# A graph layer with routed experts: the table of normed nodes kept in plain fp32 instead of three bf16 parts

## The chip, the cores and the metric

The kernel runs on one core of one Trainium2 chip. The time is the device time of one launch, in microseconds (us). Before the change it is 1744.55 us, the median of three runs (1744.52 to 1745.57). One further execution was profiled; what the profile calls the span reaches from its first to its last instruction.

## The reference, cut to what matters

6250 nodes with 256 features each; 100,000 edges, sorted by destination; eight experts with 256 x 1024 and 1024 x 256 weights. All of it is fp32.

```python
def _layernorm(x, axis=-1, eps=1e-05):
    return (x - mean) / jnp.sqrt(var + eps)

def gnn(x, edge_index, weight, bias):          # x is the normed input
    src, dst = edge_index
    summed = segment_sum(x[src], dst, n)
    deg = segment_sum(ones(src), dst, n)
    agg = summed / jnp.maximum(deg, 1.0)[:, None]
    out = jnp.concatenate([x, agg], -1) @ weight
    return out / norm(out) + bias

def ffn(h):                                    # h is the normed x
    probs = softmax(h @ gate_w + gate_b); idx = argmax(probs)
    # each token goes to its expert's next free slot (capacity C),
    # relu(buf @ w1 + b1) @ w2 + b2, back to the token, times its gate
    ...

x = x + gnn(_layernorm(x), [src, dst], ...)
x = x + ffn(_layernorm(x))
```

## The kernel before

**Setup (about the first 129 us).** The 49 blocks of 128 nodes are normed in seven groups of seven. VectorE takes the statistics (L942 to L947), norms the group (L967) and writes into `r1` what is left of each value when its upper 16 bits are taken off (L973). The upper halves of `xn` and of `r1` are two bf16 parts, copied out by ScalarE (L531, L535); the third part is what is then left, computed by GpSimd (L443). SyncE stores the three parts of a group (L249, L278) in a table in DRAM, `parts_d`, of 6250 rows of 768 bf16 values (1536 bytes). In groups 1 and 2 the edge lists (L868 to L885) and the tables of the loop (L892 to L933) are made. GpSimd's gathers start when all stores have landed (L448).

**The loop.** 49 trips, each with four quads of edges. A quad is 512 edges: four tiles of 128. For each tile GpSimd gathers the 128 source rows into `ring` (L460, an indirect DMA), which holds two quads. VectorE makes the four 128 x 128 selection matrices of a visit in one instruction (L991): a 1 where an edge's destination is a given node of the block. A visit adds up a quad's edges for one block of nodes. On TensorE each of its four tiles takes four bf16 matmuls with the same `sel` tile as weights: three of 256 columns, one for each part (L684), and one of a single column of ones (L690), which counts the edges. VectorE adds the 257 sums to `acc` (L1000). A quad has one visit, and one more where its edges cross into another block; 244 visits in all, five in nearly every trip, the earlier ones of a quad in a loop of their own ahead of its last one.

**What lies between the visits.** After each tile of a quad's last visit TensorE runs one step of a plan written out by hand (L800): steps of the node block whose sums are complete (transposes L725, the 512 x 256 linear layer L738, transposes L774, gate L780, counts L789), and from trip 8 on steps of one chunk of 128 routed rows of an expert (L731, L747, L755, L766, all fp32). The first eight trips have no chunk; in them SyncE loads the experts' weights. After the 49 trips come the last node blocks and chunks, without quads.

**What orders it.** Each engine runs its program in order. `sel_ready` and `acc_done` let a visit start (L700 to L706), `gathered` lets each pair of tiles start (L682), `ring_free`, raised by the last matmul of each tile, lets GpSimd gather again (L457), and `visit_done`, raised by the last matmul of a visit, lets VectorE add and select again (L1020, L1029, L1034). `sel` and `ps_q` have two buffers. A visit that is not its quad's last uses the buffers of the visit before it. In VectorE's trip (L1237 and on) the chains of routing, expert result and new row follow these waits in order.

```python
for part in range(NPART):
    mm = pe.matmul(ps[:, 0:D], sel[:, s, j, :], ring[..., part * D:(part + 1) * D], ...)
if final:
    mm.then_inc(ring_free, 1)
mm = pe.matmul(ps[:, D:AW], sel[:, s, j, :], ones_bf[:, :], ...)
```

## Time and profile before

| | |
|---|---|
| Median of the runs | 1744.55 us |
| Span of the profiled execution | 1742.4 us |
| TensorE, matmul records | 1183.2 us busy, 68% |
| VectorE / ScalarE / GpSimd | 898.6 / 469.4 / 922.7 us busy |
| Mean granted TensorE clock | 0.898 of 2.4 GHz |
| Three stages: setup / 49 trips / the rest | to 129 / 129 to about 1550 / to 1742 us |

The profiled execution's span lies 2.2 us below the median of the runs. Busy time is the time covered by records of work; register, branch and semaphore instructions are not counted. An fp32 matmul stands in the records as two matmuls and two weight loads, a bf16 one as one of each. Starts of matmuls are measured, their ends are modelled, so matmuls are best priced by the distance from one start to the next.

### The profile page before, as it was taken

What the parts mean: (1) busy time and instruction counts of PE and PEld (TensorE: products, weight loads), DVE (VectorE), ACT (ScalarE), POOL (GpSimd) and SP (SyncE); (2) the same over time, 40 slices, a digit from 0 to 9 for tenths busy, and PEclk for the clock granted to TensorE, in tenths of its full rate; (3) what the DMA queues carried; (4) which work ended last, traced back from release to release, by engine and by line L of the source; (5) the groups of instructions that cost most, each with busy time, mean ns of one, the idle gap of its engine ahead of it and who ended that gap; (6) DMA issues with size and microseconds to landing.
All of it is one profiled execution on the core that took longest, in us unless ns stands there. A gap on an engine that the chain in (4) does not pass through costs nothing.

```text
span 1742.4 us, 32300 instructions
## 1 busy us (share of the span) xinstructions
PE 1183.2 (68%) x6813; PEld 838.8 (48%) x6814; DVE 898.6 (52%) x3823; ACT 469.4 (27%) x1362; POOL 922.7 (53%) x939
## 2 busy tenths in 40 slices
PE   0105566677777777777777776877677777777785
PEld 0004444455555555555555554645455655554553
DVE  5753444455555545454555554554555545554443
ACT  2221111122222222222222322223222222233432
POOL 4136656656666656555656655565556665640110
PEclk9998676789999989998989998999998899888998
DMA  7736667554545444544445444444454544431111
GB/s 236 235 134 205 185 215 232 185 160 131 147 136 146 135 131 132 149 121 134 136 118 139 126 138 115 134 127 140 114 143 121 146 120 137 124 103 34 38 42 38
DMA packets 126810, 238.77 MB, mean 137 GB/s; under 512 B 21263, under 2 KB 85126, under 8 KB 126792
## 3 DMA queue, kind: packets, MB, share of 16 engines
q0 software_dynamic: 55808, 160.87, 32.7%
q1 hardware_dynamic: 70984, 77.72, 14.1%
q14 instruction: 14, 0.11, 0.0%
q8 instruction: 4, 0.07, 0.0%
HBM read 207.46 MB, written 39.29 MB: 142 GB/s over the span
## 4 chain that ended last, share of the span: by engine, by line
PE 28%; issue 19%; DVE 17%; another core or an unknown queue 11%; DVEq 10%; DMA 7%; ACT 4%; POOL 2%; SPq 2%; ACTq 0%; POOLq 0%
PE ps_q L684 10%; PE ps_h L747 5%; PE ps_b L766 5%; PE ps_a L738 3%; DVEq L1252 3%; DVEq L1060 2%; DMA ring<-parts_d,idx 2%; DVE sel L991 2%; PE ps_a L725 2%; DMA b_b<-in_L_ffn_b 2%; DMA out<-ys,node_i 1%; PE ps_t L755 1%; DVE acc L1000 1%; ACT cat_t L580 1%
## 5 line engine op out<-in xcount | busy, mean ns | idle before, releaser
L460 POOL DMA_INDIRECT ring<-parts_d,idx x784 | 763.0, 973 | 541.1 <-PE ps_q L684 277.9
L684 PE MATMUL ps_q<-ring,sel 128*128 128x256 bf16 x2928 | 506.0, 299 | 245.0 <-DMA ring<-parts_d,idx 96.7
L684 PEld LDWEIGHTS ps_q<-ring,sel 128*128 128x128 bf16 x2928 | 270.4, 106 | 416.8 <-issue 242.2
L766 PE MATMUL ps_b<-w_sb,hid_t 128*128 x864 | 264.6, 441 | 124.2 <-issue 71.2
L991 DVE SCALAR_TENSOR_TENSOR sel<-lane,block,dst_t 128x512 bf16<-128x512 bf16 x245 | 184.4, 753 | 197.4 <-issue 116.2
L766 PEld LDWEIGHTS ps_b<-w_sb,hid_t 128*128 128x128 f32 x864 | 169.6, 214 | 161.6 <-issue 141.5
L747 PE MATMUL ps_h<-w_sb,hid_t 128*128 x432 | 213.6, 622 | 5.7 <-ACT hid_t L583 5.7
L1000 DVE TENSOR_TENSOR acc<-acc,ps_q 128x257 f32 x245 | 103.3, 422 | 178.3 <-issue 57.3
L690 PE MATMUL ps_q<-ones_bf,sel 128*128 128x1 bf16 x976 | 170.8, 175 | 0.0
L738 PE MATMUL ps_a<-gw_sb,cat_t 128*128 128x256 f32 x416 | 136.3, 459 | 19.3 <-ACT cat_t L580 15.6
L604 ACT ACTIVATE hid_t<-ps_t,b_t 128x128 f32<-128x128 f32 x432 | 117.8, 382 | 55.5 <-remote 40.1
L515 ACT ACTIVATE sm<-sm 128x1 f32<-128x1 f32 x104 | 21.1, 203 | 358.3 <-DVE sm L1113 192.0
L690 PEld LDWEIGHTS ps_q<-ones_bf,sel 128*128 128x128 bf16 x976 | 105.0, 108 | 21.0
L478 POOL DMA_INDIRECT out<-ys,node_i x55 | 57.2, 1041 | 108.6 <-DVEq L1060 94.9
L598 ACT ACTIVATE hid<-ps_h 128x512 f32<-128x512 f32 x108 | 62.5, 596 | 193.7 <-PE ps_h L747 142.1
L470 POOL DMA_INDIRECT disp_d<-row,slot x53 | 60.2, 1136 | 90.9 <-issue 53.1
L747 PEld LDWEIGHTS ps_h<-w_sb,hid_t 128*128 128x128 f32 x432 | 76.3, 195 | 66.2 <-issue 65.2
L738 PEld LDWEIGHTS ps_a<-gw_sb,cat_t 128*128 128x128 f32 x416 | 84.0, 223 | 35.3 <-ACT cat_t L580 20.5
L755 PE MATMUL ps_t<-ident,hid 128*128 128x128 f32 x432 | 69.5, 284 | 30.0 <-ACT hid L598 25.7
L755 PEld LDWEIGHTS ps_t<-ident,hid 128*128 128x128 f32 x432 | 46.8, 141 | 46.0 <-ACT hid L598 33.3
L580 ACT ACTIVATE cat_t<-ps_a 128x512 f32<-128x512 f32 x52 | 31.0, 597 | 129.8 <-remote 64.7
L591 ACT ACTIVATE hid_t<-ps_a 128x256 f32<-128x256 f32 x52 | 19.9, 383 | 161.6 <-PE ps_a L738 91.4
(180 smaller groups left out, 1296.1 us busy)
## 6 DMA issues: line engine op xcount, KB each, us to landing
w_sb<-in_L_ffn_w SPq DMA_DIRECT2D x32, 512.0 KB
ring<-parts_d,idx POOLq DMA_INDIRECT x784
disp_d<-row SPq DMA_DIRECT2D x1, 8450.0 KB
parts_d<-w_sb SPq DMA_DIRECT2D x6, 1344.0 KB, 5.8
xs<-disp_d SPq DMA_DIRECT2D x55, 130.0 KB
ys<-disp_d SPq DMA_DIRECT2D x55, 130.0 KB
b_b<-in_L_ffn_b SPq DMA_DIRECT2D x55, 128.0 KB
xb<-in_x SPq DMA_DIRECT2D x51, 128.0 KB
```

The source lines that it names most:

```text
L460: pool.indirect_dma_start(ring[:, (k % 2) * TQ + j, :], None, parts_d[:, :], bass.IndirectOffsetOnAxis(ap=idx[:, k * TQ + j:k * TQ + j + 1 ...
L470: pool.indirect_dma_start(disp_d[:, :], bass.IndirectOffsetOnAxis(ap=slot[0:rows, 0:1], axis=0), row[0:rows, :], None, bounds_check=EX * S ...
L598: act.activation(hid[:, h * 512:(h + 1) * 512], ps_h[:, h * 512:(h + 1) * 512], ACT.Copy).then_inc(hid_ready, 1)
L604: done = act.activation(hid_t[:, j, :], ps_t[:, j, :], ACT.Relu, bias=b1_t[:, ds(e * JF + j, 1)])
L684: mm = pe.matmul(ps[:, 0:D], sel[:, s, j, :], ring[:, (k % 2) * TQ + j, part * D:(part + 1) * D], start=(j == 0 and part == 0), stop=(j == ...
L690: mm = pe.matmul(ps[:, D:AW], sel[:, s, j, :], ones_bf[:, :], start=False, stop=(j == TQ - 1), skip_group_check=True)
L738: last_ = pe.matmul(ps_a[:, 0:KD, :], cat_t[:, k, :], gw_sb[:, k, :], start=(k == 0), stop=(k == 2 * KD - 1))
L747: last_ = pe.matmul(ps_h[:, h * 512:(h + 1) * 512], xc_t[:, k, :], w1_sb[:, k, ds(expert[0] * F + h * 512, 512)], start=(k == 0), stop=(k ...
L755: last_ = pe.transpose(ps_t[:, j, :], hid[:, j * P:(j + 1) * P], ident[:, :])
L766: last_ = pe.matmul(ps_b[:, 0:D], hid_t[:, j, :], w2_sb[:, j, ds(expert[0] * D, D)], start=(j == 0), stop=(j == JF - 1))
L991: dve.scalar_tensor_tensor(out=sel[:, s, :, :], in0=lane[:, :].rearrange("p (j m) -> p j m", j=1).to_broadcast((P, TQ, P)), scalar=block0[ ...
L1000: dve.tensor_tensor(to, to, ps_q[s][:, 0:AW], ALU.add).then_inc(acc_done, 1)
```

## The change

The table in DRAM becomes `xn_d`, 6250 rows of 256 fp32 values (1024 bytes), stored straight from `xn`. `r1`, the two copies of ScalarE and GpSimd's subtraction are gone, with their semaphores; VectorE waits for the store of two groups before (`xn_out`) ahead of norming into the same buffer. `ring` is fp32, 257 columns wide; the last column is set to 1.0 once. `sel` is fp32. A tile takes one fp32 matmul of 257 columns; the last tile of a visit takes one of 256 columns and a second one of one column, which ends the accumulation of the count. `acc` is cleared ahead of the loop on GpSimd without waits in between.

```diff
-    parts_d = nc.dram_tensor("parts_d", (N, NPART * D), BF16, kind="Internal").ap()
+    xn_d = nc.dram_tensor("xn_d", (N, D), FP32, kind="Internal").ap()
-        ring = sb("ring", [P, 2 * TQ, NPART * D], BF16)
+        ring = sb("ring", [P, 2 * TQ, AW], FP32)
-        sel = sb("sel", [P, 2, TQ, P], BF16)
+        sel = sb("sel", [P, 2, TQ, P], FP32)
...
@@ sync
-                sp.wait_ge(low_done, g + 1)
-                sp.wait_ge(hi_copied, g + 1)
+                sp.wait_ge(xn_ready, g + 1)
...
@@ gpsimd
-            pool.memset(ones_bf[:, :], 1.0).then_inc(pool_step, 1)
+            pool.memset(ring[:, :, D:AW], 1.0).then_inc(pool_step, 1)
...
-                pool.memset(acc[:, g * AC:(g + 1) * AC], 0.0)
-                pool.wait_ge(r1_ready, g + 1)
-                if g >= 2:
-                    pool.wait_ge(parts_out[s], 16 * (g // 2))
-                pool.tensor_tensor(... third part ...).then_inc(low_done, 1)
+                pool.memset(acc[:, g * AC:(g + 1) * AC], 0.0).then_inc(acc_clear, 1)
...
-                        ring[:, (k % 2) * TQ + j, :], None, parts_d[:, :],
+                        ring[:, (k % 2) * TQ + j, 0:D], None, xn_d[:, :],
...
@@ tensor, visit
-                    for part in range(NPART):
-                        mm = pe.matmul(ps[:, 0:D], sel[:, s, j, :],
-                                       ring[:, (k % 2) * TQ + j, part * D:(part + 1) * D],
-                                       start=(j == 0 and part == 0), stop=(j == TQ - 1 and part == NPART - 1),
-                                       skip_group_check=True)
+                    width = AW if j < TQ - 1 else D
+                    mm = pe.matmul(ps[:, 0:width], sel[:, s, j, :], ring[:, (k % 2) * TQ + j, 0:width],
+                                   start=(j == 0), stop=(j == TQ - 1), skip_group_check=True)
                     if final:
                         mm.then_inc(ring_free, 1)
-                    mm = pe.matmul(ps[:, D:AW], sel[:, s, j, :], ones_bf[:, :], start=False,
-                                   stop=(j == TQ - 1), skip_group_check=True)
                     if j == TQ - 1:
+                        mm = pe.matmul(ps[:, D:AW], sel[:, s, j, :],
+                                       ring[:, (k % 2) * TQ + j, D:AW],
+                                       start=False, stop=True, skip_group_check=True)
                         mm.then_inc(visit_done, 1)
@@ vector, setup
                 if g >= 2:
-                    dve.wait_ge(hi_copied, g - 1)
-                    dve.wait_ge(low_done, g - 1)
+                    dve.wait_ge(xn_out[s], 16 * (g // 2))
...
-                dve.tensor_tensor(r1[s][:, :], xn[s][:, :], ... upper halves ...,
-                                  ALU.subtract).then_inc(r1_ready, 1)
+            dve.wait_ge(acc_clear, NG)
```

## Rows read from the trace of the kernel before

**Rows 1.** The page: granted clock by slice, and the chain that ended last
```profile
PEclk9998676789999989998989998999998899888998
PE 28%; issue 19%; DVE 17%; another core or an unknown queue 11%; DVEq 10%; DMA 7%; ACT 4%; POOL 2%; SPq 2%; ACTq 0%; POOLq 0%
```

**Rows 2.** Busy time by stage: stretch, length, PE, PEld, DVE, ACT, POOL, clock, DMA
```profile
143.00:359.10 216.10, 134.08 (x801) 97.33 (x802) 97.28 (x388) 34.32 (x108) 131.67 (x136) 0.72 0.64 203
359.10:1540.10 1181.00, 886.86 (x5364) 635.37 (x5361) 622.51 (x2720) 329.03 (x1000) 711.26 (x720) 0.92 0.47 133
```

**Rows 3.** The same view for single trips of the loop, same columns
```profile
1065.20:1100.20 35.00, 23.33 (x138) 17.34 (x136) 15.54 (x68) 8.69 (x28) 18.18 (x20) 0.80 0.40 113
1185.50:1213.50 28.00, 20.82 (x135) 14.68 (x135) 15.44 (x68) 8.20 (x25) 18.41 (x19) 1.00 0.46 132
1334.20:1362.70 28.50, 22.94 (x138) 16.87 (x135) 15.40 (x68) 8.54 (x27) 17.93 (x18) 0.88 0.48 134
1422.40:1452.30 29.90, 24.19 (x135) 17.00 (x135) 15.57 (x68) 8.26 (x26) 15.54 (x17) 0.83 0.41 115
```

**Rows 4.** Timeline of PE, full clock: start, length, line, operation
```profile
1123.87 0.59 PE L780 MATMUL ps_b<-gatew_sb,cat_t 128*128 128x8 f32 x4
1124.42 0.49 PE L684 MATMUL ps_q<-ring,sel 128*128 128x256 bf16 x3
1124.77 0.49 PE L684 MATMUL ps_q<-ring,sel 128*128 128x256 bf16 x3
...
1129.15 1.11 PE L738 MATMUL ps_a<-gw_sb,cat_t 128*128 128x256 f32 x4
1130.10 0.49 PE L684 MATMUL ps_q<-ring,sel 128*128 128x256 bf16 x3
```

**Rows 5.** Timeline of PE at the half clock
```profile
196.74 2.08 PE L738 MATMUL ps_a<-gw_sb,cat_t 128*128 128x256 f32 x4 [0.24 <-ACT cat_t L580]
198.61 0.85 PE L684 MATMUL ps_q<-ring,sel 128*128 128x256 bf16 x3
...
218.26 0.80 PE L684 MATMUL ps_q<-ring,sel 128*128 128x256 bf16 x3
218.93 0.38 PE L684 MATMUL ps_q<-ring,sel 128*128 128x256 bf16 x1
```

**Rows 6.** Costliest groups of the page: gathers and two weight loads
```profile
L460 POOL DMA_INDIRECT ring<-parts_d,idx x784 | 763.0, 973 | 541.1 <-PE ps_q L684 277.9
L684 PEld LDWEIGHTS ps_q<-ring,sel 128*128 128x128 bf16 x2928 | 270.4, 106 | 416.8 <-issue 242.2
L738 PEld LDWEIGHTS ps_a<-gw_sb,cat_t 128*128 128x128 f32 x416 | 84.0, 223 | 35.3 <-ACT cat_t L580 20.5
L991 DVE SCALAR_TENSOR_TENSOR sel<-lane,block,dst_t 128x512 bf16<-128x512 bf16 x245 | 184.4, 753 | 197.4 <-issue 116.2
```

**Rows 7.** Timelines of PE and DVE at the end of one trip
```profile
1142.69 0.17 PE L690 MATMUL ps_q<-ones_bf,sel 128*128 128x1 bf16 x1
1145.29 1.13 PE L766 MATMUL ps_b<-w_sb,hid_t 128*128 x4 [1.79 <-issue]
...
1149.12 0.42 DVE L1000 TENSOR_TENSOR acc<-acc,ps_q 128x257 f32 x1 [2.81 <-remote]
```

**Rows 8.** Who waited for whom from 340 to 1540 us: total, times, longest
```profile
PE ps_q L684 <- DMA ring<-parts_d,idx: 21.6, 34, 2.2
```

**Rows 9.** Timeline of the setup, all engines
```profile
44.16 1.23 DVE L872 SCALAR_TENSOR_TENSOR w_sb<-w_sb 98x1024 f32<-98x1024 f32 x1
...
113.59 2.03 DVE L973 TENSOR_TENSOR w_sb<-w_sb 128x1792 f32<-128x1792 f32 x1
115.70 3.17 POOL L443 TENSOR_TENSOR w_sb<-w_sb 128x1792 bf16<-128x1792 f32 x1 [5.07 <-DVE w_sb L973]
119.31 0.40 SPq L278 DMA_DIRECT2D parts_d<-w_sb  x1
128.88 1.04 POOL L460 DMA_INDIRECT ring<-parts_d,idx  x1 [10.00 <-issue]
```

More of the change, by code:

```diff
@@ L129, in gnn_moe_layer @@
         xn = [carve(w1_flat, (2 + s) * XW, XW) for s in range(2)]
-        r1 = [carve(w1_flat, (4 + s) * XW, XW) for s in range(2)]
-        parts = [carve(w2_flat, s * NPART * XW // 2, NPART * XW // 2).bitcast(BF16) for s in range(2)]
-        at = NPART * XW
+        at = 0
         dst_i = carve(w2_flat, at, 2 * QE).bitcast(I32)
@@ L168, in gnn_moe_layer @@
         xn_ready = sem("xn_ready")
-        r1_ready = sem("r1_ready")
-        hi_copied = sem("hi_copied")
-        low_done = sem("low_done")
-        parts_out = [sem(f"parts_out{s}") for s in range(2)]
+        acc_clear = sem("acc_clear")
+        xn_out = [sem(f"xn_out{s}") for s in range(2)]
         stage_f = sem("stage_f")
@@ L246, in load_x, with store_xn @@
                                  ).then_inc(xin_in[g % 3], 16)
-            def store_parts(g, s, blocks):
-                sp.dma_start(parts_d[ds(g * (XG * P), blocks * P), :].rearrange("(b p) d -> p b d", p=P),
-                             parts[s][:, 0:blocks * NPART * D].rearrange("p (b d) -> p b d", d=NPART * D)
-                             ).then_inc(parts_out[s], 16)
+            def store_xn(g, s, blocks):
+                sp.dma_start(xn_d[ds(g * (XG * P), blocks * P), :].rearrange("(b p) d -> p b d", p=P),
+                             xn[s][:, 0:blocks * D].rearrange("p (b d) -> p b d", d=D)
+                             ).then_inc(xn_out[s], 16)
             load_x(0)
@@ L271, in _ @@
                     load_x(g + 3)
-                sp.wait_ge(low_done, g + 1)
-                sp.wait_ge(hi_copied, g + 1)
+                sp.wait_ge(xn_ready, g + 1)
                 if g < NG - 1:
-                    store_parts(g, s, XG)
+                    store_xn(g, s, XG)
                 else:
-                    store_parts(g, s, XG - 1)
-                    sp.dma_start(parts_d[(NB - 1) * P:N, :],
-                                 parts[s][0:LAST, (XG - 1) * NPART * D:XG * NPART * D]).then_inc(parts_out[s], 16)
+                    store_xn(g, s, XG - 1)
+                    sp.dma_start(xn_d[(NB - 1) * P:N, :],
+                                 xn[s][0:LAST, (XG - 1) * D:XG * D]).then_inc(xn_out[s], 16)
                 if g == 0:
@@ L285, in _ @@
                                  ).then_inc(x1_out, 16)
[L287 to L288 removed]
+            sp.wait_ge(xn_out[0], 16 * (NG // 2 + 2))
+            sp.wait_ge(xn_out[1], 16 * (NG // 2))
             sp.wait_ge(valid_ready, 1)
@@ L437, in _ @@
             for g in range(NG):
[L438 to L449 removed]
+                pool.memset(acc[:, g * AC:(g + 1) * AC], 0.0).then_inc(acc_clear, 1)
+            pool.wait_ge(xn_out[0], 16 * (NG // 2 + 2))
+            pool.wait_ge(xn_out[1], 16 * (NG // 2))
             last, end, t_reg = (pool.alloc_register(n) for n in ("last_node_slot", "chunk_end", "slot"))
@@ L526, in _ @@
                             ).then_inc(ln1_ready, 1)
-                view = parts[s][:, :].rearrange("p (b k d) -> p b k d", k=NPART, d=D)
-                act.wait_ge(xn_ready, g + 1)
-                if g >= 2:
-                    act.wait_ge(parts_out[s], 16 * (g // 2))
-                act.activation(view[:, :, 0, :],
-                               xn[s][:, :].bitcast(BF16).rearrange("p (b d t) -> p b d t", d=D, t=2)[:, :, :, 1],
-                               ACT.Copy)
-                act.wait_ge(r1_ready, g + 1)
-                act.activation(view[:, :, 1, :],
-                               r1[s][:, :].bitcast(BF16).rearrange("p (b d t) -> p b d t", d=D, t=2)[:, :, :, 1],
-                               ACT.Copy).then_inc(hi_copied, 1)
                 if g == 1:
```

15 lines of the change are left out of this document (removed).

## Prediction, made before the change was run

> **What bounds the kernel now.** First the chain that ended last and the granted clock, on the page [rows 1]. No engine has more than 28% of the chain, and 11% of it, about 190 us, stands under "another core or an unknown queue" on a kernel with one core: time in which an engine waits and the profile knows no releaser. Then the busy times by stage [rows 2]. From 359 to 1540 us lie 40 trips with a chunk: 29.5 us each, TensorE busy 22.2 of them, GpSimd 17.8, VectorE 15.6, ScalarE 8.2, and DMA at 47%. So TensorE is the fullest engine, but it has 7.3 us of gaps in each trip. The eight trips before have no chunk: 27.0 us each, TensorE busy 16.8, its clock at 0.72.
>
> Next single trips [rows 3], whose ends I put at the first L738 record of each trip. A trip at the full clock took 28.0 us with 20.8 busy, gaps 7.2. One with 2.1 us more of TensorE time, because part of it ran at 1.2 GHz, took 28.5, and its gaps were 5.6. One with 3.4 more took 29.9, gaps 5.7. So extra TensorE work first eats gaps, down to about 5.6 us, and then lengthens the trip. The trip of 35.0 us, with 11.7 of gaps, shows that some trips are long for a reason that isn't TensorE work.
>
> That reason shows in the timelines at the end of a trip [rows 7]. The last matmul of a visit starts at 1142.69 us, and VectorE needs nothing but its completion to add it up (L1034), yet the add runs at 1149.12, after 2.81 us of idle time put down to "remote". TensorE's completion seems to become visible six microseconds late. GpSimd waits on the same engine's `ring_free` for 277.9 us in all [rows 6]. I can't name the mechanism, and take it as something that stays.
>
> **The change, part by part.** TensorE first, by starts. Bf16 tiles that follow each other, three parts and the count, are 0.35 us apart (1124.42, 1124.77); two fp32 matmuls of 256 columns with a fresh weight tile each take 0.95 us (1129.15 to 1130.10), 0.475 us apiece [rows 4]. A tile becomes 0.125 us longer, with the single-column matmul already in the 0.35. At the half clock it is 0.67 against 1.87 / 2 = 0.935, so 0.265 longer [rows 5]. The column 257 is below what these rows resolve. The second matmul of a visit's last tile has its nearest row in the gate, two fp32 matmuls of 8 columns in 0.55 us, 0.275 each [rows 4]; I take 0.275 for it, twice that at the half clock. One visit at the full clock: 4 x 0.125 + 0.275 = 0.775 us, and five visits 3.9 us. Over 244 visits that is 189 us of TensorE work, if all were at 2.4 GHz.
>
> The profile's own price for an fp32 matmul can be held against a page. The Trainium skill, in FP8 and Floating Point Precision, TensorE Precision Notes, has true fp32 go through the array in four passes. By that a tile of 257 columns would take 428 ns at 2.4 GHz, and by the page the tile grows by some 0.08 us, the visits' tiles by 78 us instead of 122 in all. The rows' distance of 0.475 us is from the same form of instruction in this kernel, so the sum stays with it. The same skill, in TensorE: Matmul & The Clock Gate, Weight-path perf modes, says that the fast weight load isn't available for fp32 weights, which speaks against this change; the trace agrees, as the next sentence shows.
>
> A weight load of fp32 is 223 ns in the mean against 106 for bf16 [rows 6]. Where matmuls follow each other it lies under the matmul before and is in the 0.475. Where a visit starts after a wait it is bare: 0.1 us, some three times a trip, 0.3 us.
>
> In a trip with a chunk the clock is 0.92, so 16% of the time is at the half clock [rows 2], and a tile grows by 0.125 + 0.16 x 0.14 = 0.147 us. 20 x 0.147 + 5 x 0.3 + 0.3 = 4.7 us. With gaps at the 5.6 of the fuller trips the trip would be 22.2 + 4.7 + 5.6 = 32.5 us. If a fuller TensorE kept the full clock throughout, it would be 20.8 + 3.9 + 0.3 + 5.6 = 30.6. I take 31.7, near the middle: 2.2 us more, times 40 is **+88 us**. Bounds: 30.6, +44 us; and gaps that don't shrink, +4.7 a trip, +188 us.
>
> In the eight trips ahead more than half of the time is at the half clock: 20 x 0.21 + 5 x 0.4 = 6.2 us more in each, against gaps of (216.1 - 134.1) / 8 = 10.3 [rows 2]. I take 1.5 us of it as visible, **+12 us**; bounds 0 and +50.
>
> Setup. VectorE's subtraction (2.03 us) goes in all seven groups. In the first group it lay beside the wait for a load of x; six are on the path, 12.2 us. GpSimd's third part of the last group, 3.17 us, goes [rows 9]. From the last store to the first gather were 9.6 us, and the store shrinks by a third: 1 us. ScalarE's copies ran beside these and leave nothing on the path. The new wait of VectorE, for the store of two groups before, has behind it only the norming of that group; stores are now a third smaller and about one group (8 us) old by then, so I cost it at nothing, and 2 to 3 us a group if that cover fails. On SyncE the store now waits for `xn_ready` alone, and the load of the next x ahead of it isn't moved. Sum **-16 us**; bounds -20 and -5, the second if the loads of x become what comes last.
>
> Gathers. They carry 1024 bytes a row instead of 1536. TensorE waited for them 21.6 us from 340 to 1540 us [rows 8]; that is the most to be won there. I take **-5 us**, since GpSimd's 973 ns for each gather [rows 6] lie on the way too, and I know of no row that makes them shorter with shorter rows.
>
> At nothing: VectorE's selection writes fp32. It takes 753 ns for 512 columns [rows 6], 1.5 ns a column; an instruction of the same kind all in fp32 took 1.23 us for 1024 [rows 9], 1.2 ns a column, so the wider type costs nothing there; were it to cost, 245 selections and the short visits that wait for them are where it would show. Clearing `acc` in one go and the ones in `ring` are a few us of GpSimd early in the setup, beside VectorE's statistics.
>
> Sum: -16 + 12 + 88 - 5 = +79 us on the span of 1742.4, so 1821.4, and with the 2.2 us between the span and the median **1824 us**.
>
> **The rivals.**
> *Faster: the late completions get rarer.* They occur in the stretch in which visits and gathers run. A tile now brings TensorE two matmuls and two loads in the records instead of four and four, and a gather has a third fewer bytes; if either is what delays its completions, the 190 us of the chain without a known releaser shrink. It decides from about 80 us on, 40% of them; with two thirds gone, 1824 - 125 = about 1700 us. For it: GpSimd's and VectorE's waits for TensorE are large [rows 6, 7]. Against it: nothing in the rows ties them to bytes or to the number of matmuls.
> *Covered: the gaps take all of it.* The step from 20.8 to 22.9 us of busy time cost 0.5 us of a trip [rows 3]. If it goes on like this the loop gains 10 to 30 us and the setup gives 16 back: 1730 to 1755 us. Against it: the next step, to 24.2, cost 1.4 us for 1.25.
> *In series: the gaps don't shrink.* They then hang on waits that come after the visits, like VectorE's of rows 7. +188 in the 40 trips, some +30 in the eight, -20: about 1940 us.
>
> **How the numbers follow.** The forecast's case has 0.63, the late completions 0.13 (about 1700), covered 0.12 (0.05 of it faster by over 0.2%, 0.03 within, 0.04 slower), in series 0.12 (about 1940). 0.2%, 3.5 us, is about what a measurement of this kernel can tell from no change. Faster 0.18, same 0.03, slower 0.79. The range of 1735 to 1935 us leaves out the first rival and the upper half of the last, 0.19.
>
> **What would show it.** The groups of `ps_q` by form: fp32 matmuls of 257 columns 0.47 to 0.48 us apart for each pair of records at the full clock, and records of one column. Busy TensorE per trip of 25 to 27 us, gaps of 5 to 6, periods of 31 to 32.5. The first gather at about 113 us instead of 128.9. A clock of the loop at or above 0.92. DMA share of the loop down from 0.47. The prediction is wrong if the trip's gaps fall below 4 us or stay over 7, if "another core or an unknown queue" moves by more than a few per cent of the span, or if the setup still waits for a load or store.

## The result, and the profile after the change

The changed kernel takes 1784.85 us, the median of six executions; with the kernel before on the same chip the ratio is 1.018, with an interval of 1.012 to 1.025. A second set on another chip gave 1768.7 us and a ratio of 1.014 (1.012 to 1.016). The ratios here and below leave out executions more than 1.5% above the fastest of their kernel, two of the six in the second set, so they need not equal the quotient of the medians, 1.023 in the first set. The change makes the kernel slower, as predicted, but by 24 us (the second ratio) to 40 us (the medians of the first set) and not by 79. The executions are spread from 1759 to 1799 us, and the time goes with the granted clock: 1761 us at 0.893 and 0.895, 1785 to 1787 us at 0.878 to 0.887 in the first set, 1758.6 us at 0.897 and 1799.2 us at 0.881 in the second. The profiled execution is one of the shorter: 1761.0 us, span 1759.2. It stands against the span of 1742.4 us before, so its rows explain 17 us.

The page, parts 1, 2 and 4, of the kernel after:

```profile
PE 1290.9 (73%) x5349; PEld 968.1 (55%) x5350; DVE 883.5 (50%) x3816; ACT 448.9 (26%) x1348; POOL 899.6 (51%) x932
...
PEclk9988787898898998888899888989989999988998
...
PE 25%; issue 21%; DVE 17%; another core or an unknown queue 13%; DVEq 11%; DMA 6%; ACT 3%; SPq 2%; ACTq 1%; POOL 0%; POOLq 0%
```

TensorE has 108 us more busy time than before and fewer records. Still it has a smaller share of the chain than in [rows 1], and the clock has more eights in the middle. The same stages as in [rows 2], cut at the first L709 record of a trip (L738 before), and two single trips, for [rows 3]:

```profile
111.30:333.30 222.00, 152.43 (x564) 120.89 (x563) 98.02 (x392) 33.78 (x106) 133.10 (x137) 0.76 0.51 161
333.30:1561.50 1228.20, 974.70 (x4162) 738.87 (x4161) 623.57 (x2713) 332.14 (x1000) 710.43 (x720) 0.90 0.32 93
...
1320.70:1348.00 27.30, 21.77 (x105) 16.67 (x103) 15.53 (x68) 7.67 (x23) 15.91 (x17) 1.00 0.34 98
1348.00:1383.90 35.90, 25.91 (x104) 19.88 (x105) 15.59 (x68) 8.70 (x28) 18.58 (x19) 0.86 0.28 77
```

This gives the account of the 17 us. The loop starts 31.7 us earlier (111.3 against 143.0). The first eight trips take 222.0 us instead of 216.1, +6. The 40 trips with a chunk take 30.7 us each instead of 29.5, +47. What comes after them is 4.6 us shorter. -32 + 6 + 47 - 5 = +16, which is the difference of the spans, 16.8 us, within rounding. In a trip with a chunk TensorE's busy time grew by 2.2 us (24.4 against 22.2), its gaps shrank from 7.3 to 6.3, and the clock fell from 0.92 to 0.90. The lower clock is the small part of the growth: TensorE was busy at 1.2 GHz for 4.7 us of a trip instead of 4.1, and as work takes twice as long there ([rows 4] and [rows 5]), that is 0.3 us, an estimate. The rest of the 2.2 us is more work; trips wholly at 2.4 GHz show 1.4.

The groups of the page that answer to [rows 6]:

```profile
L444 POOL DMA_INDIRECT ring<-xn_d,idx x784 | 770.5, 983 | 602.3 <-issue 356.5
L656 PE MATMUL ps_q<-ring,sel 128*128 128x257 f32 (+1 forms) x1952 | 663.7, 449 | 234.0 <-DVE sel L958 67.7
L656 PEld LDWEIGHTS ps_q<-ring,sel 128*128 128x128 f32 x1952 | 392.9, 221 | 350.3 <-issue 197.3
L958 DVE SCALAR_TENSOR_TENSOR sel<-lane,block,dst_t 128x512 f32<-128x512 bf16 x245 | 184.1, 752 | 242.3 <-issue 125.7
```

A gather with a third fewer bytes takes GpSimd as long as before (983 against 973 ns), and VectorE's selection with fp32 output too (752 against 753): the selection's term, put at nothing, holds, and for the gathers no shorter instruction had been counted on.

Why a tile cost less than predicted is in the timeline of TensorE at the full clock. Columns: start, length, line, operation.

```profile
1504.07 0.68 PE L656 MATMUL ps_q<-ring,sel 128*128 128x257 f32 x2
1504.58 0.17 PE L760 MATMUL ps_b<-hot,tri 128*128 128x8 bf16 x1
...
1506.44 0.60 PE L656 MATMUL ps_q<-ring,sel 128*128 128x257 f32 x2
1506.87 0.60 PE L726 MATMUL ps_t<-ident,hid 128*128 128x128 f32 x4
1507.31 0.60 PE L656 MATMUL ps_q<-ring,sel 128*128 128x257 f32 x2
1507.74 0.60 PE L726 MATMUL ps_t<-ident,hid 128*128 128x128 f32 x4
1508.18 0.60 PE L656 MATMUL ps_q<-ring,sel 128*128 128x256 f32 x2
1508.62 0.28 PE L661 MATMUL ps_q<-ring,sel 128*128 128x1 f32 x2
...
1102.64 0.60 PE L656 MATMUL ps_q<-ring,sel 128*128 128x257 f32 x2
1103.08 1.03 PE L737 MATMUL ps_b<-w_sb,hid_t 128*128 x4
1103.94 0.60 PE L656 MATMUL ps_q<-ring,sel 128*128 128x256 f32 x2
```

A tile of 257 columns is 0.43 to 0.44 us from the next start (1506.44 to 1506.87, 1507.31 to 1507.74), not 0.475. Two fp32 matmuls of 256 columns are 0.86 us (1103.08 to 1103.94), where [rows 4] had 0.95. The prediction took its price from that 0.95.

### The profile page after: what moved, and what is told of

It reads as the page before. It is cut to its first block, busy times and chain, and to the rows that moved or that the text cites. A ratio compares the mean times of both kernels' runs of the same rounds, so it can differ in the third digit from the quotient of the medians.

```text
span 1759.2 us, 29322 instructions
## 1 busy us (share of the span) xinstructions
PE 1290.9 (73%) x5349; PEld 968.1 (55%) x5350; DVE 883.5 (50%) x3816; ACT 448.9 (26%) x1348; POOL 899.6 (51%) x932
## 3 DMA queue, kind: packets, MB, share of 16 engines
q0 software_dynamic: 43264, 109.49, 21.6%
## 4 chain that ended last, share of the span: by engine, by line
PE 25%; issue 21%; DVE 17%; another core or an unknown queue 13%; DVEq 11%; DMA 6%; ACT 3%; SPq 2%; ACTq 1%; POOL 0%; POOLq 0%
PE ps_q L656 12%; PE ps_b L737 3%; DVEq L1027 3%; PE ps_h L718 3%; PE ps_a L709 2%; DVEq L1219 2%; PE ps_a L696 2%; DMA b_b<-in_L_ffn_b 2%; DVE sel L958 2%; DMA out<-ys,node_i 1%; DMA w_sb<-in_x 1%; DVE acc L967 1%; PE ps_b L751 1%; DMA ring<-xn_d,idx 1%
## 5 line engine op out<-in xcount | busy, mean ns | idle before, releaser
L444 POOL DMA_INDIRECT ring<-xn_d,idx x784 | 770.5, 983 | 602.3 <-issue 356.5
L656 PE MATMUL ps_q<-ring,sel 128*128 128x257 f32 (+1 forms) x1952 | 663.7, 449 | 234.0 <-DVE sel L958 67.7
L656 PEld LDWEIGHTS ps_q<-ring,sel 128*128 128x128 f32 x1952 | 392.9, 221 | 350.3 <-issue 197.3
L958 DVE SCALAR_TENSOR_TENSOR sel<-lane,block,dst_t 128x512 f32<-128x512 bf16 x245 | 184.1, 752 | 242.3 <-issue 125.7
L737 PE MATMUL ps_b<-w_sb,hid_t 128*128 x864 | 238.2, 408 | 42.4 <-issue 22.6
L454 POOL DMA_INDIRECT disp_d<-row,slot x53 | 55.5, 1048 | 147.0 <-DVE slot L1057 95.4
L709 PE MATMUL ps_a<-gw_sb,cat_t 128*128 128x256 f32 x416 | 118.8, 413 | 15.7 <-ACT cat_t L552 10.5
L661 PEld LDWEIGHTS ps_q<-ring,sel 128*128 128x128 f32 x488 | 104.3, 214 | 18.5
L709 PEld LDWEIGHTS ps_a<-gw_sb,cat_t 128*128 128x128 f32 x416 | 85.5, 210 | 38.4 <-ACT cat_t L552 18.4
L726 PEld LDWEIGHTS ps_t<-ident,hid 128*128 128x128 f32 x432 | 53.3, 146 | 65.8 <-ACT hid L570 51.7
L661 PE MATMUL ps_q<-ring,sel 128*128 128x1 f32 x488 | 73.6, 220 | 0.0
```

Source lines behind the costliest of these rows:

```text
L444: pool.indirect_dma_start(ring[:, (k % 2) * TQ + j, 0:D], None, xn_d[:, :], bass.IndirectOffsetOnAxis(ap=idx[:, k * TQ + j:k * TQ + j + 1] ...
L454: pool.indirect_dma_start(disp_d[:, :], bass.IndirectOffsetOnAxis(ap=slot[0:rows, 0:1], axis=0), row[0:rows, :], None, bounds_check=EX * S ...
L656: mm = pe.matmul(ps[:, 0:width], sel[:, s, j, :], ring[:, (k % 2) * TQ + j, 0:width], start=(j == 0), stop=(j == TQ - 1), skip_group_check ...
L661: mm = pe.matmul(ps[:, D:AW], sel[:, s, j, :], ring[:, (k % 2) * TQ + j, D:AW], start=False, stop=True, skip_group_check=True)
L709: last_ = pe.matmul(ps_a[:, 0:KD, :], cat_t[:, k, :], gw_sb[:, k, :], start=(k == 0), stop=(k == 2 * KD - 1))
L726: last_ = pe.transpose(ps_t[:, j, :], hid[:, j * P:(j + 1) * P], ident[:, :])
```

## The experiments

Edits are given against the kernel named. Spans, first gathers and trips are read as above; "trip" is the mean of the 40 trips with a chunk, cut at the first matmul of the linear layer.

### Do the gathered bytes count?

```diff
 two_parts, against before
-    parts_d = nc.dram_tensor("parts_d", (N, NPART * D), ...)
+    parts_d = nc.dram_tensor("parts_d", (N, 2 * D), ...)
-    ring[:, (k % 2) * TQ + j, part * D:(part + 1) * D]
+    ring[:, (k % 2) * TQ + j, min(part, 1) * D:(min(part, 1) + 1) * D]
 wide_rows, against after
-    xn_d = nc.dram_tensor("xn_d", (N, D), FP32, ...)
+    xn_d = nc.dram_tensor("xn_d", (N, 320), FP32, ...)
```

The 64 further columns of wide_rows are ones, stored in the setup, gathered, and read by nothing.

> The kernel before, but the table and the gathers hold two of the three bf16 parts (1024 bytes a row, as after the change); the third matmul of a tile reads the second part once more, so the low part of the sums is missing. TensorE's instructions are those of before. Theory A (the loop's growth of 47 us after the change is TensorE's fp32 form alone, gather bytes count for nothing): trips with a chunk stay at 29.5 us, the time is 1744 less the 1 to 5 us of the shorter stores. Theory B (fewer gathered bytes gave a gain that hid part of a larger cost of the fp32 form): trips of 28.5 to 29.2 us, 1700 to 1732 us, and DMA's waits of TensorE below 10 us.

> The kernel after, but a gathered row has 1280 bytes instead of 1024 (64 columns of ones that nothing reads), half way back to the 1536 of before; the store of these columns lies in the setup and may add up to 10 us to it. Theory A (bytes count for nothing): trips with a chunk stay at 30.7 us. Theory B (bytes count): 30.9 to 31.2 us, 8 to 20 us more over the 40 trips.

two_parts: 1741.4 us, ratio 0.999 (0.997 to 1.001), trips of 29.45 us. wide_rows: 1774.0 us, ratio 1.019 (1.014 to 1.023), trips of 30.8. Their loops in the view by stage, two_parts first, then wide_rows:

```profile
361.20:1539.10 1177.90, 890.61 (x5361) 633.64 (x5360) 623.82 (x2718) 327.61 (x999) 713.88 (x719) 0.93 0.34 97
```

```profile
341.10:1573.80 1232.70, 972.71 (x4162) 737.24 (x4161) 624.01 (x2714) 332.34 (x1000) 712.08 (x720) 0.90 0.39 110
```

A third fewer bytes took the DMA share from 0.47 to 0.34 and TensorE's waits for gathers from 21.6 to 2.6 us, and a trip lost 0.07 us, 3 us over the loop. wide_rows, with a quarter more bytes than after, has trips 0.1 us longer. So bytes count for next to nothing in the loop, in either kernel, and its growth is left to TensorE's fp32 form and to what follows from it. In the setup they do count: two_parts has its first gather at 126.59 us, 2.3 earlier than before.

### What holds up TensorE's completions?

```diff
 free2, against after
-    if final:
-        mm.then_inc(ring_free, 1)
+    if final and j % 2 == 1:
+        mm.then_inc(ring_free, 2)
 paced_load, against after, behind each pair of gathers
+    pool.load([pause], ends[0:1, 0:1])
```

> The kernel after, but TensorE raises ring_free by 2 on every second tile instead of by 1 on each: GpSimd waits for pairs anyway. TensorE's completions that carry an update fall from five to three in a quad's last visit. If the number of updates is what holds TensorE's completions up, VectorE's and ScalarE's waits put down to remote fall (sel 93, hid 80 us between 333 and 1530 us) and trips get 0.5 to 1 us shorter: 1730 to 1765 us. If GpSimd's issue of gathers is what holds them, nothing changes: 1755 to 1790 us.

> The kernel after, but GpSimd reads one word into a register after each pair of gathers, which makes it pause for 1 to 2 us eight times in a trip. Theory G (gathers that GpSimd issues back to back hold up TensorE's completions, a pause lets them out): waits put down to remote shrink by half or more, gaps of TensorE in a trip fall from 6.2 to 5 us or less, trips of 29 to 30 us, 1700 to 1760 us. Rival (gathers are merely later): TensorE's waits for gathers grow, trips of 31 us or more, 1790 us or more.

free2 took 1757.4 to 1791.5 us, the spread of the changed kernel; VectorE's waits for `sel` put down to remote were 122.2 us in it and ScalarE's for `hid` 111.8, more than the 99.3 and 80.2 of after. But free2's profile is of its longest execution, and that of after_again, as long (1790.6 against 1791.5 us), has 134.3 and 96.6: no gain by fewer updates is seen, and the number of updates isn't shown as the cause. paced_load took 1775.1 us, ratio 1.019 (1.015 to 1.023), with 96.7 and 82.3 us. It doesn't test its theory, because GpSimd didn't pause. Its gathers still follow each other at 1.25 us, with the 0.30 us in between that they have in after:

```profile
1010.11 0.94 POOL L445 DMA_INDIRECT ring<-xn_d,idx  x1 [0.30 <-issue]
1011.36 0.94 POOL L445 DMA_INDIRECT ring<-xn_d,idx  x1 [0.30 <-issue]
```

So gathers issued back to back stay an untested rival. What such a late completion looks like, in the timeline of the kernel after, behind the matmuls of 1507 to 1509 us shown above:

```profile
1515.70 1.14 ACT L576 ACTIVATE hid_t<-ps_t,b_t 128x128 f32<-128x128 f32 x4 [6.95 <-remote]
1515.87 0.42 DVE L967 TENSOR_TENSOR acc<-acc,ps_q 128x257 f32 x1 [2.70 <-remote]
1516.44 0.94 POOL L444 DMA_INDIRECT ring<-xn_d,idx  x1 [2.84 <-remote]
1516.98 1.52 PE L737 MATMUL ps_b<-w_sb,hid_t 128*128 x4 [3.09 <-ACT hid_t L576]
```

ScalarE and VectorE get work that TensorE had started by 1508.6 us released seven microseconds later, within 0.2 us of each other, GpSimd gets its next gather 0.6 us after that, and then TensorE itself waits 3.09 us for ScalarE. Its cause stays open.

These waits didn't stay as they were. Over the 40 trips VectorE's waits for `sel` put down to remote were 56.6 us before, 99.3 after, and 57.3 in between_again, and ScalarE's for `hid` 39.0, 80.2 and 24.0; between_again is the kernel after with twelve short matmuls added to a trip, tried further down. The changed kernel has more of these waits, and the faster one of its variants has fewer.

### The setup: where do 31 us come from?

```diff
 clear_first, against before (GpSimd)
             for g in range(NG):
-                s = g % 2
                 pool.memset(acc[:, g * AC:(g + 1) * AC], 0.0)
+            for g in range(NG):
+                s = g % 2
 sub_back, against after (VectorE, each group)
+    dve.tensor_tensor(r1[s], xn[s], ...upper halves of xn[s]..., ALU.subtract).then_inc(r1_ready, 1)
 low_back, against after: sub_back's line, and on GpSimd and SyncE, each group
+    pool.wait_ge(r1_ready, g + 1)
+    pool.tensor_tensor(out=..., in0=r1[s], in1=..., op=ALU.subtract).then_inc(low_done, 1)
+    sp.wait_ge(low_done, g + 1)
```

> The kernel before, with one edit: GpSimd clears acc in one go before the seven groups instead of one seventh ahead of each group's third part. Theory S (a GpSimd clear of 1.6 us beside VectorE's short instructions holds these up, 1.6 us in each of the later groups, and this is part of why the setup shrank by 31 us where 16 were expected): the first gather comes at 119 to 124 us instead of 128.9, the time is 1733 to 1741 us. Rival (the clears cost nothing, the 15 extra us are all from the removed arithmetic and the store): first gather at 127 us or later, time as before.

> The kernel after, with VectorE's subtraction of 2.0 us in each group put back (its result is read by nobody). The prediction's term for it was 12.2 us for six groups on the path. If that term was right, the first gather comes at 110 to 111 us instead of 98.2, and the other 18 us of the setup's gain come from GpSimd's and the stores' side. If the short VectorE instructions were what gave, it comes below 106.

> The kernel after, with VectorE's subtraction and GpSimd's third part put back in each group (results read by nobody) and SyncE's store waiting for the third part again. With VectorE's subtraction alone the first gather came at 107.2 us instead of 98.2. The prediction's term for the rest was 3.2 us (the last group's third part). Theory S (GpSimd's work beside VectorE's short instructions holds these up in every group): first gather at 113 to 119 us. Rival (only the last group's third part is on the path): 110 to 111 us.

The first gathers of the kernel after, sub_back, low_back and clear_first, each from its timeline; before had it at 128.88 us [rows 9]:

```profile
98.20 1.24 POOL L444 DMA_INDIRECT ring<-xn_d,idx  x1 [78.80 <-issue]
```

```profile
107.21 1.50 POOL L447 DMA_INDIRECT ring<-xn_d,idx  x1 [87.81 <-issue]
```

```profile
121.56 1.04 POOL L458 DMA_INDIRECT ring<-xn_d,idx  x1 [7.62 <-issue]
```

```profile
124.25 1.05 POOL L461 DMA_INDIRECT ring<-parts_d,idx  x1 [10.04 <-issue]
```

So of 30.7 us the clears between the groups were worth 4.6 (128.88 to 124.25), ScalarE's copies and the longer stores 2.7 (124.25 to 121.56), what low_back adds to sub_back 14.4 (121.56 to 107.21) and what sub_back adds to after 9.0. Both of the last lie outside what had been expected of them. In two places these steps mix causes. From the last store to the first gather are 9.6 us in clear_first (store at 114.66) and 7.1 in low_back (at 114.43), so 2.5 of the 2.7 are the longer store. And the last store of sub_back doesn't wait for its group's subtraction, while those of low_back and of the kernel before do. So some 2 of the 14.4 us belong to the subtraction, which makes about 11 for it and about 12 for GpSimd's third part. clear_first alone makes the kernel before faster: 1741.9 against 1749.2 us, ratio 0.996 (0.995 to 0.998). sub_back took 1789.2 us and low_back 1805.6, one execution each.

Why the clears and the third part cost more than their own time is seen where they lie beside VectorE. First the kernel before, around the norming of the fifth group, then low_back, from its second group to its last:

```profile
88.29 1.80 DVE L947 TENSOR_SCALAR w_sb<-w_sb 128x7 f32<-128x7 f32 x1
88.46 1.60 POOL L439 MEMSET acc<- 128x1799 f32 x1
88.47 1.62 DVE L846 TENSOR_TENSOR w_sb<-w_sb 128x7 f32<-128x7 f32 x1
...
90.18 0.17 DVE L848 TENSOR_TENSOR w_sb<-w_sb 128x7 f32<-128x7 f32 x1
```

```profile
40.36 3.66 DVE L854 CAST w_sb<-w_sb 98x1024 f32<-98x1024 int32 x1
...
64.15 2.66 DVE L884 TENSOR_TENSOR w_sb<-w_sb 1x103 f32<-1x103 f32 x1
...
101.93 3.17 POOL L441 TENSOR_TENSOR w_sb<-w_sb 128x1792 bf16<-128x1792 f32 x1 [5.63 <-DVE w_sb L958]
102.00 3.12 DVE L833 TENSOR_TENSOR w_sb<-w_sb 128x7 f32<-128x7 f32 x1
...
110.77 3.17 POOL L441 TENSOR_TENSOR w_sb<-w_sb 128x1792 bf16<-128x1792 f32 x1 [5.67 <-DVE w_sb L958]
111.70 0.15 DVE L1035 COPY sm<-node_id 128x1 f32 x1 [0.79 <-issue]
...
114.43 0.40 SPq L276 DMA_DIRECT2D xn_d<-w_sb  x1
```

An arithmetic instruction of VectorE on seven columns takes 0.17 us alone, 1.6 us beside GpSimd's clear and 3.12 us beside its third part: it ends when GpSimd's does. It is not only the short ones: in low_back a cast of 1024 columns took 3.66 us instead of sub_back's 0.68, and an addition of 103 columns 2.66 instead of 0.25, both beside a third part. And not every short one is held up: the copy of one column at 111.70 us, inside the last third part, took 0.15, and the statistics of the sixth group ran beside one at their usual length. With the 2.95 us of the seven columns the three held-up instructions make 8.3 us, and the third part of the last group, ahead of the last store, 3.2 more. With the 2 us of subtraction that is 13.5 of the 14.3 us by which the last store came later (100.09 us in sub_back, 114.43 here).

### Single-column matmuls, and the clock

```diff
 bf16_between and between_again, against after, behind tiles 0 to 2 of a quad's last visit
                     if j < len(between):
+                        if j < TQ - 1:
+                            pe.matmul(ps[:, 300:301], ones[:, :], ones[:, 0:1], start=True, stop=True, ...)
                         between[j]()
 f32_between: the same with ident[:, :], ident[:, 0:1]
```

> The kernel after, with one bf16 matmul of a single column put behind each of the first three tiles of a quad's last visit, ahead of the step that follows: 12 a trip, results unused. Theory B (where an fp32 matmul follows a bf16 one on TensorE it starts 0.08 to 0.09 us later, which the kernel before paid ahead of each fp32 step and again nobody after): the fp32 steps' groups are again 0.08 us longer (L709's of four records 0.95 instead of 0.86 us, transposes 0.47 instead of 0.44) and TensorE's busy time of a trip grows by more than the 12 single matmuls' own spacing. Rival (the shorter groups of after come from something else): groups stay at 0.86 and 0.44 us.

> The same as the kernel with bf16 matmuls put in, but the added single-column matmuls are fp32 (12 a trip). It is its control, and prices a single-column fp32 matmul, which the prediction put at 0.275 us. Theory B: the fp32 steps' groups stay at 0.86 and 0.44 us, and each added matmul takes about 0.14 us from start to next start. Rival: 0.22 to 0.28 us each, and groups as long as with the bf16 ones.

> The kernel with twelve single-column bf16 matmuls a trip once more, now timed in rounds: one execution of it took 1738 us with a granted clock of 0.926, against 1761 to 1787 us at 0.88 to 0.895 for the kernel after. Theory C (how much of a trip TensorE spends at 1.2 GHz decides between such times; the added matmuls keep the clock up): every run has a clock above 0.91 and lies at 1730 to 1750 us. Rival (that one execution was chance): runs spread over 1755 to 1790 us, clock 0.88 to 0.90.

At the full clock f32_between has:

```profile
1001.55 0.60 PE L656 MATMUL ps_q<-ring,sel 128*128 128x257 f32 x2
1001.98 0.28 PE L667 MATMUL ps_q<-ident 128*128 128x1 f32 x2
1002.12 1.11 PE L739 MATMUL ps_b<-w_sb,hid_t 128*128 x4
1003.07 0.60 PE L656 MATMUL ps_q<-ring,sel 128*128 128x257 f32 x2
```

and between_again:

```profile
1002.07 0.60 PE L656 MATMUL ps_q<-ring,sel 128*128 128x257 f32 x2
1002.50 0.17 PE L667 MATMUL ps_q<-ones 128*128 128x1 bf16 x1
1002.53 0.64 PE L728 MATMUL ps_t<-ident,hid 128*128 128x128 f32 x4
1003.00 0.60 PE L656 MATMUL ps_q<-ring,sel 128*128 128x257 f32 x2
...
1010.94 1.11 PE L739 MATMUL ps_b<-w_sb,hid_t 128*128 x4
1011.89 0.60 PE L656 MATMUL ps_q<-ring,sel 128*128 128x257 f32 x2
```

In both kernels the group behind a single-column matmul is as long as before the change: 0.95 us (1002.12 to 1003.07; 1010.94 to 1011.89), and the transposes 0.47. Theory B, that the switch from bf16 to fp32 costs it, falls: the fp32 column does it as well. What they share is a matmul of one column in front. The reading that fits is that it is too short to cover the weight load behind it (221 ns in the groups above), which a tile of 257 columns in front covers. The added matmul itself is 0.14 us in fp32 (1001.98 to 1002.12) and 0.03 in bf16 (1002.50 to 1002.53).

The twelve added matmuls also make the kernel faster: 1726.9 us for between_again, ratio to before 0.993 (0.989 to 0.997), clocks of 0.911 to 0.919. bf16_between, the same kernel on another chip, took 1737.9 us and f32_between 1758.8, one execution each, at 0.926 and 0.924. The loops of between_again and of bf16_between:

```profile
341.30:1525.20 1183.90, 977.60 (x4643) 729.54 (x4641) 622.25 (x2715) 333.26 (x1000) 716.99 (x720) 0.94 0.34 97
```

```profile
338.00:1539.00 1201.00, 977.96 (x4643) 724.40 (x4641) 625.33 (x2719) 332.05 (x1000) 715.09 (x720) 0.95 0.33 95
```

In between_again TensorE has the busy time of after (977.6 against 974.7 us) although work was added, because less of it runs at 1.2 GHz: a clock of 0.94 against 0.90. In the 40 trips the clock fell from 2.4 to 1.2 GHz 26 times, 45 times in after and 41 in before. Counted over the single trips, after ran 5 of 40 wholly at the full clock, between_again 13. Those trips take 27.8 us in the mean in after and 27.9 in between_again, against 28.4 in the five such trips of before, although TensorE is busy for 22.2 us in them in after instead of 20.8. The changed kernel's loop is longer in its trips with much time at 1.2 GHz: 26 trips with more than 6.5 us of it, at 31.9 us each, where before had 14, at 31.0.

That is an order, not yet a cause. With equal busy time, the whole gain of between_again over after lies in TensorE's gaps: 5.2 us a trip instead of 6.3. The time at 1.2 GHz fell together with the waits put down to remote (see above), and a trip that is long for its waits can lower the clock as well as the other way round. Nor does a higher clock alone bring the gain: bf16_between has 0.95 and a loop 17 us longer than between_again, and its eight trips wholly at the full clock take 29.9 us in the mean. clear_first has a clock of 0.94 in its loop and is 4 us shorter there than before at 0.92.

### Filling TensorE's gaps, and using them

One gap comes in nearly every trip: TensorE reads the next trip's table into registers and issues no matmul for nearly 2 us ([rows 7], 1.79 us idle; after, 1.68):

```profile
1509.99 0.67 PE L656 MATMUL ps_q<-ring,sel 128*128 128x257 f32 x2
1512.34 1.13 PE L737 MATMUL ps_b<-w_sb,hid_t 128*128 x4 [1.68 <-issue]
```

```diff
 fill_quads (on after), before_fill (on before): ahead of the reading
+    for _ in range(4):
+        pe.matmul(ps_q[1][:, AW:512], ident[:, :], gw_sb[:, 0, 0:512 - AW], start=True, stop=True, ...)
 load_late (on after), clear_late (on clear_first)
-    [steps((quads, load_quads), (chunk, down, (2, 3))),
+    [steps((chunk, down, (2, 3)), (quads, load_quads)),
 best_f32: after, bf16_between's edit, load_late's, and two of fill_quads' matmuls
 best_bf16: clear_late and two of fill_quads' matmuls
 between_late: after, bf16_between's edit and load_late's
```

> The kernel after, with four fp32 matmuls of 255 columns (1.7 us, results unused) ahead of the step in which TensorE reads the next trip's quad table into registers. In that reading of about 2 us TensorE's array stands idle, in every trip. Theory C: the added work lies under the reading, so trips get no longer by it, and with the gap filled the half-clock time of a trip falls from 5.8 us to 4 or less: 1735 to 1755 us. Rival (the clock doesn't follow from this gap): half-clock time stays at 5 to 6.5 us and the time at 1760 to 1795 us. If the matmuls aren't hidden at all, +1.7 us a trip, above 1800 us.

> The kernel before, with the four fp32 matmuls of 255 columns (results unused) ahead of TensorE's reading of the quad table. Theory C (filled gaps keep TensorE's clock up, in either kernel): half-clock time of a trip falls from 4.9 us to 3 to 4 us, clock of the run above 0.91, 1715 to 1735 us. Rival (only the kernel after has clock to win back, since before has the many bf16 matmuls of one column already): clock 0.90, time as before or some us longer, 1740 to 1760 us.

> The kernel after, but TensorE's reading of the quad table stands behind the two fp32 matmuls of L737 of the same step instead of ahead of them: 0.86 us of the step's work then runs during the reading, and nothing is added. Theory C: a trip gets 0.4 to 0.9 us shorter by the smaller gap and more by a higher clock: 1725 to 1755 us. Rival (the gap is covered by waits that end later anyway): trips stay at 30.7 us, 1760 to 1787 us.

> The kernel before with acc cleared ahead of the seven groups and the reading of the quad table behind the two fp32 matmuls of L766. The first alone gave a ratio of 0.996 against the kernel before. If the gap of 1.8 us ahead of L766 in every trip is on the path, trips fall from 29.5 to 28.6 to 29.1 us and the time to 1700 to 1725 us; if it is covered, the time stays at 1735 to 1745 us.

> The kernel after with three edits together: the twelve single-column bf16 matmuls a trip, the reading of the quad table behind the two fp32 matmuls of its step, and two fp32 matmuls of 255 columns ahead of it. Theory C: clock at 0.91 or above and trips of 28.7 to 29.3 us, 1690 to 1725 us, faster than both kernels. Rival (the three have the same gain, one is enough): 1720 to 1735 us.

> The kernel before with three edits together: acc cleared ahead of the groups, the reading of the quad table behind the two fp32 matmuls of its step, and two fp32 matmuls of 255 columns ahead of it. Without the added matmuls its granted clock was 0.882 and its ratio to before 0.992. Theory C: the clock returns to 0.90 or above, trips of 28.3 to 28.9 us, 1690 to 1720 us. Rival (the added matmuls are not hidden here, the reading being covered already): 1730 us or more.

> The kernel after, unchanged, on the chip of the next kernel. Its earlier profile is one of its shorter executions (1761 us, clock 0.893). If the times split again into about 1760 and 1785 us, the longer ones should have the lower clock (0.88 to 0.887 against 0.893 or more), and more half-clock time in a trip.

> The kernel after with the twelve single-column bf16 matmuls a trip and the later reading of the quad table, without the added matmuls of 255 columns. If the two gains add up (0.7 to 1.1 us a trip by the first, 0.2 by the second), trips of 29.3 to 29.6 us and a ratio to before of 0.982 to 0.990. If filled gaps and work behind the reading give the same thing once, the ratio is that of the single-column matmuls alone, 0.993, or above.

| kernel | median us | ratio to before | interval | trip us | loop clock |
|---|---|---|---|---|---|
| after_again | 1768.7 | 1.014 | 1.012 to 1.016 | 31.4 | 0.88 |
| fill_quads | 1727.9 | 0.992 | 0.987 to 0.996 | 30.4 | 0.93 |
| load_late | 1750.2 | 1.003 | 0.999 to 1.008 | 30.5 | 0.89 |
| between_late | 1730.0 | 0.992 | 0.990 to 0.995 | 30.0 | 0.92 |
| best_f32 | 1732.1 | 0.991 | 0.988 to 0.994 | 30.0 | 0.93 |
| before_fill | 1767.1 | 1.013 | 1.010 to 1.016 | 29.7 | 0.96 |
| clear_late | 1725.9 | 0.992 | 0.988 to 0.996 | 29.3 | 0.90 |
| best_bf16 | 1745.3 | 1.000 | 0.998 to 1.001 | 29.7 | 0.91 |

Trip and clock are of the one profiled execution, which for fill_quads, load_late and after_again was one of the longer and for before_fill the shortest of four; the medians are of all. One execution of load_late took 6385.6 us, and one of the kernel before in the set of after_again and between_late 5846.7; nothing on record explains them, and no ratio has them in it. On their common chip after_again took 1768.7 us and between_late 1730.0. The chip of fill_quads, load_late and clear_late was also that of between_again. There the kernel before took 1742.3 us, with a spread of 32 us.

In the changed kernel filler pays: fill_quads computes nothing more, has 1.15 us more TensorE time in a trip (1020.7 against 974.7 us over 40), and is 0.8% faster than before while after is 1.4 to 1.8% slower. In the kernel before the same filler costs 1.3%, though the clock rises from 0.92 to 0.96:

```profile
369.00:1556.70 1187.70, 937.73 (x5684) 671.87 (x5681) 624.53 (x2722) 331.57 (x1000) 718.18 (x720) 0.96 0.47 132
```

That is 1.27 us more of TensorE a trip for a loop 6.7 us longer than in [rows 2], and the eight trips ahead of it 9 us longer. So theory C as I had put it, that filled gaps pay in either kernel, fell. A higher clock can be a gain only where the work that raises it is less than what it gives back; that before had less to give back fits this, but isn't shown by it. clear_late shows the other side: without filler, with a lower clock (0.90), it is as fast as the best. Its table is read behind 0.86 us of work that is needed anyway; its loop is 6.4 us shorter than that of clear_first, one profile each (1170.9 against 1177.3 us). Adding filler to it (best_bf16) takes that away again. The gains don't add up in the changed kernel either: best_f32 and between_late are no faster than between_again or fill_quads within their intervals. clear_late, between_again, fill_quads, between_late and best_f32 beat both kernels, by 0.7 to 0.9% of before; their intervals overlap.

after_again repeats the relation of time and clock in after: 1758.6 us at 0.897, 1761.8 at 0.889, 1767 to 1770 at 0.885 to 0.887, 1790.6 and 1799.2 at 0.881. Not two levels but a spread, ordered by the clock. Which of the two causes the other isn't told by this, and not by between_again and fill_quads either: the TensorE work added in them changes the clock, the order in time and the remote waits at once.

## Why the prediction was right or wrong, point by point

- **What failed.** The direction came, slower by over 0.2% at 0.79. The size didn't: +79 us on the span was forecast, and the profiled execution has +17, the medians +40. The failed step is the price of a visit, "4 x 0.125 + 0.275 = 0.775 us": at the full clock a trip's five visits, 3.9 us by it, brought 1.4 us more busy time, and over all 40 trips the busy time grew by 2.2 us where 4.7 were forecast. That made the term of the 40 trips 88 us where 47 were measured; with 2.2 in place of 4.7 and the prediction's own visible share it would have been about 41. The setup term failed too, -16 where -31 was measured. The 1785 us (1769 on the second chip) lie 39 us below the forecast, between it and the rival "covered" (1730 to 1755).
- **Setup, -16 forecast, -31 measured: wrong in its parts.** VectorE's subtraction was priced at 12.2 us and is about 11, which is right. GpSimd's third part was priced at 3.2, the last group's, and is about 12; the shorter store, priced at 1, is 2.5; the clears between the groups, put at nothing as "a few us of GpSimd early in the setup", are 4.6. The failed step is "GpSimd's third part of the last group, 3.17 us, goes": it counted only what stands in the chain by name, and not what the third part did to VectorE's instructions beside it. Those that take 1.6 us and more instead of 0.17 stood in the trace of before, and I hadn't looked for a VectorE instruction beside a GpSimd one. The new wait for a store cost nothing, as costed: no instruction of L937 has a wait for one in the timeline of the later groups. A load of x was waited for once, 0.87 us in the sixth group.
- **A visit's growth, 0.775 us forecast: the mis-sized term.** The tile's price came from two fp32 matmuls that stood behind a single-column matmul, whose short run left 0.085 us of the next weight load bare. Behind wide matmuls a tile is 0.435 us: a growth of 0.08, not 0.125. The single-column fp32 matmul is 0.14, not 0.275; the nearest row, with eight columns, was itself a group behind a short matmul. And the removed count matmuls gave back what nobody had counted: 0.085 us for eleven of a trip's steps. Per trip at the full clock 20 x 0.08 + 5 x 0.14 + 5 x 0.085 (a visit's first tile where it stands behind the single column: 1504.07 to 1504.58, 0.51 us) - 11 x 0.085 = 1.8 us, with the 0.085 for each step an upper value, since transposes gain 0.035. The full-clock trips show 22.2 against 20.8, +1.4; the forecast was 3.9. True fp32 goes through the array in four passes by the Trainium skill (FP8 and Floating Point Precision, TensorE Precision Notes), from which a tile of 257 columns is 428 ns at 2.4 GHz, an estimate. The prediction set this aside for the row; the measured 0.43 to 0.44 us agrees with it. An estimate and a row that differ by 10% would have been reason to look for a second row.
- **Gaps shrink to 5.6 and the rest is visible: near in size, by luck.** 6.3 us remain. Of 2.2 us more busy time 1.2 were visible, 0.53 of it; the forecast took 2.2 of 4.7, 0.47. But it isn't one rule for all trips. In the five trips wholly at the full clock nothing was visible, as the rival "covered" had it: 22.2 us busy, gaps of 5.6, 27.8 us against 28.4. With trips of 26.8 to 29.0 us among the five that is a weak count. In the 26 trips with much time at 1.2 GHz gaps of 6.9 us stayed. The 5.6 had been read from three trips of before; its 14 trips with more than 6.5 us at 1.2 GHz have gaps of 7.8 us in the mean.
- **"A fuller TensorE keeps the full clock", taken as a bound: wrong in sign.** I had expected 0.92 or more; the loop's clock fell to 0.90, and 0.88 in the longer executions. By the estimate above the lower clock itself adds 0.3 us to TensorE's busy time in a trip, 12 us of work in 40 trips, so by itself it isn't the whole of the 47 us. Whether long trips lower the clock or the clock makes trips long is open.
- **First eight trips +12, gathers -5:** +6 and, by two_parts, 3 us for the bytes. Right in sign, within their bounds. The 5 us by which the rest behind the trips is shorter were in no term.
- **Late completions, taken as something that stays.** In the chain they are 13% against 11%, but in the 40 trips VectorE's waits of this kind for `sel` grew from 56.6 to 99.3 us and ScalarE's for `hid` from 39.0 to 80.2. The experiments didn't name the cause, and one of the two, paced_load, didn't do what it was built for.

## What to carry to other kernels

Price a matmul from a row whose predecessor is like the one it will have: behind a matmul of one column a group of fp32 matmuls was 0.085 us longer here. Where two engines' instructions overlap in a timeline, compare the short one's length with its usual length; a removal can give back more than its own time. Look in an experiment's trace whether the edit did what it was meant to do, before reading its time. And where the granted clock flickers, filling a gap, or better, moving needed work into it, is worth a try, with the kernel's own filler-free version timed beside it: here the same filler gained in one kernel and lost in the other.

## What was not expected of the hardware

- VectorE instructions of seven columns took as long as the GpSimd clear (1.6 us) or subtraction (3.1 us) beside them, against 0.17 us alone. A cast of 1024 columns went from 0.68 to 3.66 us; a copy of one column stayed at 0.15.
- With twelve added single-column matmuls a trip, results unused, the loop's clock was 0.94 instead of 0.90, and the kernel went from 1.4 to 1.8% above before to 0.7% below it. Shortly ahead of the falls to 1.2 GHz TensorE had been idle for 1.8 us in one piece in the kernel before, for 2.0 to 2.4 in after and for 1.9 in between_again (medians over the falls in the 40 trips); why such falls are rarer with a few short matmuls spread over the trip, 26 instead of 45, is not settled. They may shift the trips' timing as well as fill them.
- A third fewer gathered bytes changed neither GpSimd's time for a gather (983 against 973 ns) nor, by more than 0.1 us, the trip.
- TensorE's completions became visible up to seven microseconds late to ScalarE, VectorE and GpSimd at nearly the same time, and no less so with fewer updates.
